# Clearing PSUM banks with a full stationary, and one value product in twelve moved from VectorE to ScalarE

## The chip, the cores and the metric

One NeuronCore of a Trainium2 chip runs the kernel. The metric is device time in microseconds of that core, from a launch to its end. Times of instructions come from one profiled execution; they count from the first instruction of its span.

## What is computed

A graph layer, an attention-like layer and a routed feed-forward layer over 1250 nodes of 512 features, with 21250 edges. The part that matters here is the graph layer, which the kernel turns into products with a dense, weighted adjacency matrix of 1250 x 1250:

```python
m = jnp.maximum(jnp.max(weighting_gate), 0.0)
exp_e = jnp.exp(weighting_gate - m)                       # one weight for each edge
row_sum = jax.ops.segment_sum(exp_e, src, num_segments=n_nodes)
atten_e = exp_e / (row_sum[src] + 1e-06)
Mfeat = source_features @ Wm + bm
out0 = jax.ops.segment_sum(atten_e[:, None] * Mfeat[dst], src, num_segments=n_nodes)
out1 = jax.ops.segment_sum(atten_e[:, None] * Mfeat[src], dst, num_segments=n_nodes)
h = jax.nn.relu(_layernorm(concatenate([out0, out1], -1) @ W1 + b1, gamma, beta))
...
x = x + _L0_gnn_ref(...) + _L0_mix_ref(...)               # then a routed feed-forward layer on top
```

## The kernel before, in words

The program is written engine by engine, each with its own instruction order, and semaphores between them. Its stages, in order: edges are sorted into buckets, and their records scattered to memory by GpSimd while the projections and the attention-like layer run on the other engines (to about 200 us); the last edges are sorted by products (L656, to 232 us); **the adjacency stage** (239 to 338 us); scaling and turning of the adjacency matrix and the products with the node features (L705, L712, L730 on); the routed feed-forward layer from 430 us on.

The adjacency stage builds 50 tiles of the matrix, each 125 source rows by 250 destination columns, and one column more for row sums. The sorted edge slots stand in 216 chunks of 128, one slot to a partition; each chunk belongs to one tile. 216 chunks are 108 pairs (PAIRS), and the pairs lie in 28 batches (BATCHES, L95): 26 of four pairs (PB), then two of two.

- **VectorE** makes the operands of a batch (L1190 to L1208): `s_one`, a one-hot of the source row (L1196), 128 columns for each chunk; `d_hot`, a one-hot of the destination column (L1200), 250 for each; and three products of `s_one` with a part of the edge's weight (L1207). The weight is split into WT = 3 parts of 16 bits (`parts[:, 2]` to `[:, 4]`), since the operands are bf16. A four-pair batch has 1024 columns in each of `s_one` and the three `s_hot`. `s_one` has two buffers, `d_hot` and `s_hot` have four (DB); VectorE waits for its own work (`one_ok`, `batch_ok`) and, from the fifth batch on, for TensorE's products of the batch four before (`chunk_ps`).
- **TensorE** takes pair by pair (L676 to L695). For each pair it first clears the bank in which a new tile begins, or an idle bank if none begins: a product of zeros with one column (L685), whose start flag makes the next products overwrite. The bank is in a register, computed from a table (`new_at`). The stationary of this product is one row of ones. Then come six products of 251 columns (L693), three weight parts for each of two chunks, into a bank that again a register gives. It waits for `batch_ok` before a batch's first product, and before a pair's clearing for `win_ok`, the copies up to the third pair before.
- **ScalarE** copies, for each pair, two tiles' worth (502 columns) out of PSUM to the matrix `adj` (L1525), to an idle place where no tile ended; the places are in registers, which are loaded anew from `at_i` once in four pairs (L1512). When all 108 copies are done VectorE sums the rows (L1213) and takes reciprocals, ScalarE (L1531) and VectorE scale the matrix, and TensorE begins to turn it (L705).

```python
pe.matmul(flat_banks[:, bass.ds(at_new, 1)], ones_row, zero_col, start=True, stop=False,
          skip_group_check=True)
...
for j in range(2):
    ...
    for i in range(WT):
        mm = pe.matmul(flat_banks[:, bass.ds(at_in, AW)], s_hot[:, n % DB, i, q, :, j],
                       d_hot[:, n % DB, q, :, j], start=False, stop=(i == WT - 1), skip_group_check=True)
```

Nothing plans the order: it is as the loops are written. The functions below hold the whole stage; the constant named `before` is a 128 x 128 matrix of 0 and 1 in 16 bits, whose first column is zero.

Of the kernel before, what the change touches and what calls it, by code (L numbers as in the profile page):

```python
# [16 lines left out]
TP, NT = 125, 10  # L17
# [84 lines left out]
def build(nc, x, edge_src, edge_dst, edge_w, consts, halves, biases, small, fold, wqkv, wp, bvt, w1f, w2f, b2f, out):  # L102
    with ExitStack() as ctx:
# [37 lines left out]
        ones_row, zero_col = half("ones")[0:1, :], half("before")[0:1, 0:1]  # L141
# [61 lines left out]
        parts = place("parts", 33728, [128, 2 + WT, NCH], BF16)  # L203
        d_hot = place("d_hot", 16064, [128, DB, PB, AW, 2], BF16)
# [101 lines left out]
        def piece(a, i):  # L306
# [21 lines left out]
        zeros_set, top_col, top_row, top_val, top_bc, top_sb, w_exp = (  # L328
            sem("zeros_set"), sem("top_col"), sem("top_row"), sem("top_val"), sem("top_bc"), sem("top_sb"), sem("w_exp"))
# [4 lines left out]
        fold_ps, fold_hi, fold_ok, foldb_ok = sem("fold_ps"), sem("fold_hi"), sem("fold_ok"), sem("foldb_ok")  # L334
# [3 lines left out]
        stat_ok, sum_ok, var_ok, std_ok, rstd_ok, xn_ok, xT_ps, xT_ok = (  # L338
            sem("stat_ok"), sem("sum_ok"), sem("var_ok"), sem("std_ok"), sem("rstd_ok"), sem("xn_ok"), sem("xT_ps"), sem("xT_ok"))
        q_ps, k_ps, v_ps, m_ps = sem("q_ps"), sem("k_ps"), sem("v_ps"), sem("m_ps")  # L340
        q_got, k_got, v_ok, m_ok = sem("q_got"), sem("k_got"), sem("v_ok"), sem("m_ok")
        top_ok, exp_ok, soft_ok, qT_ps, qT_ok, ctx_ps, ctx_ok, ctx_ok1, ctxd_zero = (
            sem("top_ok"), sem("exp_ok"), sem("soft_ok"), sem("qT_ps"), sem("qT_ok"), sem("ctx_ps"), sem("ctx_ok"),
            sem("ctx_ok1"), sem("ctxd_zero"))
# [6 lines left out]
            sem("col_ok"), sem("one_ok"), sem("batch_ok"), sem("chunk_ps"), sem("win_ok"))  # L351
        rinv_ok, even_ok, odd_ok, turn_ps, turn_a, turn_v, out_split = (
# [6 lines left out]
        var2_ok, std2_ok, x2T_ps, x2T_ok, log_ps, log_ok, lexp_ok, oh_ok, rank_ps = (  # L359
            sem("var2_ok"), sem("std2_ok"), sem("x2T_ps"), sem("x2T_ok"), sem("log_ps"),  # L360
            sem("log_ok"), sem("lexp_ok"), sem("oh_ok"), sem("rank_ps"))
        fac_ok, fac_st, tab_ok, ctab_ps, id_ok, exp_of = (
            sem("fac_ok"), sem("fac_st"), sem("tab_ok"), sem("ctab_ps"), sem("id_ok"), sem("exp_of"))
# [119 lines left out]
        def _(pe):  # L483
# [14 lines left out]
            pe.wait_ge(top_val, 1)  # L498
            pe.matmul(bank[4][0:TP, 0:1], ones[0:1, 0:TP], top[0:1, 2:3], start=True, stop=True).then_inc(top_bc, 1)
# [35 lines left out]
            def project(t):  # L535
                pe.wait_ge(xT_ok, t + 1)
                pe.wait_ge(xT_lo_ok, t + 1)
                for b, a, n, free, done in ((3, 0, D, q_got, q_ps), (4, D, D, k_got, k_ps),
# [6 lines left out]
                    if t == 0 and b == 4:  # L545
                        pe.wait_ge(foldb_ok, 1)
                    if t == 0 and b == 5:
                        pe.wait_ge(fold_ok, 2)
# [47 lines left out]
            pe.wait_ge(ctx_ok, 1)  # L596
# [79 lines left out]
            for p in range(PAIRS):  # L676
# [11 lines left out]
                if p == BATCHES[n][0]:  # L688
                    pe.wait_ge(batch_ok, n + 1)
# [1047 lines left out]
```

## Time and profile before

| | |
|---|---|
| median of 3 runs | 523.14 us (523.12 to 523.48) |
| the profiled execution | 522.98 us, span 520.7 us |
| mean granted TensorE clock over the span | 0.961 |
| TensorE products busy | 464.6 us, 89% |
| TensorE weight loads busy | 372.4 us, 72% |
| VectorE busy | 414.9 us, 80% |
| ScalarE busy | 256.7 us, 49% |
| GpSimd busy | 198.8 us, 38% |

How to read it: the span runs from the first to the last instruction; the execution's own time has 2.3 us more. Shares are means over stages with quite different limits, so a change inside one stage has to be judged by the rows of that stage. TensorE has two rows, since weight loads overlap products. A clock of 1.00 is 2.4 GHz, 0.50 is 1.2 GHz.

### The profile page before, as it was taken

To read this page: it belongs to the slowest core of one execution; us is meant where nothing else is said; L and a number is where in the kernel's file an instruction comes from. 1 tells how busy PE (TensorE), PEld (TensorE's weight loads), DVE (VectorE), ACT (ScalarE), POOL (GpSimd) and SP (SyncE) were. 2 spreads that over 40 slices of the span, in tenths; PEclk is the share of its full clock that TensorE was granted. 3 is DMA by queue.
4 is the path that set the end of the run, shared out by engine and by line. 5 is a ranking of instruction groups with operands and counts; after the bars stand their busy time and mean duration, and the time that the engine had idled before them with its cause. 6 is when DMAs were issued, how large, how long until landed. Compare 5 with 4: busy or idle time off the path is not lost.

```text
span 520.7 us, 8981 instructions
## 1 busy us (share of the span) xinstructions
PE 464.6 (89%) x2877; PEld 372.4 (72%) x2877; DVE 414.9 (80%) x793; ACT 256.7 (49%) x682; POOL 198.8 (38%) x159
## 2 busy tenths in 40 slices
PE   4189999999988999989999999989999847999992
PEld 1167878888867887967666666588988745788881
DVE  6969999999988887979999999578639857265562
ACT  0596566666661110003666666675345482466650
POOL 0088878688876888840000000000000006345322
PEclk9789999999999999999999999989999957899998
DMA  7980000000000000013000000000003992343210
GB/s 188 292 284 3 1 3 2 3 3 2 3 1 2 3 1 3 2 34 148 1 2 1 2 2 2 1 1 0 1 1 103 432 311 66 100 119 102 85 60 15
DMA packets 15840, 31.08 MB, mean 60 GB/s; under 512 B 7750, under 2 KB 8381, under 8 KB 14773
## 3 DMA queue, kind: packets, MB, share of 16 engines
q1 hardware_dynamic: 9237, 23.21, 13.3%
q0 software_dynamic: 6560, 7.32, 7.2%
q8 instruction: 25, 0.41, 0.3%
q14 instruction: 18, 0.15, 0.1%
HBM read 24.90 MB, written 7.38 MB: 62 GB/s over the span
## 4 chain that ended last, share of the span: by engine, by line
PE 40%; POOL 32%; issue 11%; DVE 8%; DMA 4%; SPq 3%; ACT 2%; DVEq 0%; POOLq 0%; ACTq 0%
POOL slots L454 31%; PE banks L693 16%; PE banks L840 6%; PE banks L532 5%; PE banks L712 3%; SPq L375 2%; PE banks L685 2%; PE banks L705 2%; PE banks L831 1%; PE banks L494 1%; DMA x_rows<-factors 1%; DVE rec L1274 1%; DVE stat L1276 1%; DMA rec<-x_rows,get_i 1%; PE banks L850 1%
## 5 line engine op out<-in xcount | busy, mean ns | idle before, releaser
L454 POOL DMA_INDIRECT slots<-record,row_i x120 | 161.6, 1346 | 68.4 <-issue 68.4
L465 POOL DMA_INDIRECT rec<-x_rows,get_i x17 | 20.0, 1176 | 207.0 <-DMA x_rows<-factors 202.1
L693 PE MATMUL banks<-d_hot,s_hot 128*128 128x251 bf16 x648 | 92.1, 276 | 0.9 <-DVE s_hot L1207 0.9
L1525 ACT ACTIVATE adj<-banks x108 | 63.7, 590 | 37.0 <-PE banks L693 36.8
L693 PEld LDWEIGHTS banks<-d_hot,s_hot 128*128 128x128 bf16 x648 | 54.4, 98 | 9.5 <-issue 1.0
L532 PE MATMUL banks<-w_hi,xT_hi 128*125 128x512 f32 (+1 forms) x160 | 59.5, 372 | 0.8 <-DVE bia L1045 0.4
L532 PE MATMUL banks<-w_hi,xT_lo 128*125 128x512 f32 (+1 forms) x160 | 58.6, 366 | 0.0
L532 PE MATMUL banks<-w_lo,xT_hi 128*125 128x512 f32 (+1 forms) x160 | 58.5, 366 | 0.0
L1207 DVE TENSOR_TENSOR s_hot<-s_one,parts 128x1024 bf16<-128x1024 bf16 (+1 forms) x84 | 51.0, 656 | 0.0
L1470 ACT ACTIVATE q_sb<-q_sb,hmax 125x64 f32<-125x64 f32 x80 | 26.7, 336 | 39.8 <-DVE hmax L1064 39.8
L532 PEld LDWEIGHTS banks<-w_hi,xT_hi 128*125 128x125 f32 x160 | 29.7, 185 | 7.1 <-issue 1.6
L532 PEld LDWEIGHTS banks<-w_hi,xT_lo 128*125 128x125 f32 x160 | 29.7, 185 | 5.6
L532 PEld LDWEIGHTS banks<-w_lo,xT_hi 128*125 128x125 f32 x160 | 29.7, 186 | 5.6
L473 POOL DMA_INDIRECT out<-o_sb,out_i x17 | 16.9, 994 | 41.4 <-DVE o_sb L1375 41.4
L1370 DVE TENSOR_TENSOR y_sb<-banks,b_sb 128x512 f32<-128x512 f32 x17 | 11.8, 691 | 26.1 <-PE banks L532 26.1
L1200 DVE TENSOR_TENSOR d_hot<-col,parts 128x2000 bf16<-128x2000 bf16 (+1 forms) x28 | 32.1, 1146 | 0.0
L656 PE MATMUL banks<-chunk_1h,row_1h 125*128 125x216 bf16 x250 | 26.0, 258 | 3.1 <-DVE row_1h L1142 2.0
L656 PEld LDWEIGHTS banks<-chunk_1h,row_1h 125*128 125x128 bf16 x250 | 23.2, 97 | 6.0 <-DVE row_1h L1142 4.5
L685 PEld LDWEIGHTS banks<-hlf 1*128 1x128 f16 x108 | 9.8, 90 | 23.6 <-issue 23.6
L1470 ACT ACTIVATE k_sb<-k_sb,hmax 125x64 f32<-125x64 f32 x80 | 26.6, 334 | 0.0
L712 PE MATMUL banks<-adj,msg 125*128 125x250 f32 x100 | 23.2, 378 | 0.0
L1496 ACT ACTIVATE xT_hi<-banks 128x500 fp32r<-128x500 f32 x10 | 5.9, 588 | 34.2 <-PE banks L617 34.2
(299 smaller groups left out, 1065.9 us busy)
## 6 DMA issues: line engine op xcount, KB each, us to landing
w_raw<-in_w2f SPq DMA_DIRECT2D x4, 1024.0 KB, 9.1
w_raw<-in_wqkv SPq DMA_DIRECT2D x3, 1024.0 KB, 18.9
rec<-in_x SPq DMA_DIRECT2D x2, 1120.0 KB
x_rows<-rec SPq DMA_DIRECT2D x10, 224.0 KB
w1a<-in_w1f SPq DMA_DIRECT2D x1, 2048.0 KB, 8.5
w1b<-in_w1f SPq DMA_DIRECT2D x1, 2048.0 KB, 16.6
b_sb<-in_b2f SPq DMA_DIRECT2D x1, 2048.0 KB, 22.2
slots<-record,row_i POOLq DMA_INDIRECT x120, 2.6
```

The lines of the kernel that those rows point to most:

```text
L454: pool.indirect_dma_start(slots, bass.IndirectOffsetOnAxis(ap=row_i[:, c:c + 1], axis=0), record[:, c, :], None).then_inc(slot_st, 16)
L465: pool.indirect_dma_start(rec_c[:, c % RING, :], None, x1_rows, bass.IndirectOffsetOnAxis(ap=get_i[:, c:c + 1], axis=0)).then_inc(ld_rec[c ...
L532: mm = pe.matmul(dst, ab, cd, start=(i == 0), stop=(i == n - 1))
L656: mm = pe.matmul(bank[1][:, k * NCH:(k + 1) * NCH], row_1h[:, n % RS, v, :, j], chunk_1h[:, n % RS, :, j], start=(n == 0 and j == 0 and v ...
L685: pe.matmul(flat_banks[:, bass.ds(at_new, 1)], ones_row, zero_col, start=True, stop=False, skip_group_check=True)
L693: mm = pe.matmul(flat_banks[:, bass.ds(at_in, AW)], s_hot[:, n % DB, i, q, :, j], d_hot[:, n % DB, q, :, j], start=False, stop=(i == WT - ...
L712: pe.matmul(hid_at(w), msg[:, t, GH:MD], adjw[:, t, w, 0:WIN], start=(t == 0), stop=False, skip_group_check=True)
L840: mm = pe.matmul(bank[1][:, 0:F], xsT[:, c % 2, k, :], w1_sb[k // 2][:, k % 2, bass.ds(e * F, F)], start=(k == 0), stop=(k == KD - 1))
L1200: dve.tensor_tensor(d_hot[:, r, 0:k, 0:WIN, :], col_2[:, :, :].unsqueeze(1).to_broadcast([128, k, WIN, 2]), values(1).to_broadcast([128, k ...
L1207: last = dve.tensor_tensor(s_hot[:, r, i, 0:k, :, :], s_one[:, n % 2, 0:k, :, :], values(2 + i).to_broadcast([128, k, CH, 2]), ALU.mult)
L1470: last = act.activation(ah, ah, ACT.Exp, bias=hmax[:, i, h:h + 1], accum_out=hsum[:, i, h:h + 1])
L1525: act.activation(adj[:, bass.ds(w, BW2)], flat_banks[0:TP, bass.ds(out_at, BW2)], ACT.Copy).then_inc(win_ok, 1)
```

## The change

1. The clearing product of each pair takes the whole 128 x 128 constant `before` as its stationary and that constant's first column, which is zero in all 128 rows, as the moving operand. It still clears, and still adds nothing.
2. For the batches 1 to 25, VectorE makes the third value product only for the first three pairs (768 of 1024 columns). ScalarE makes the fourth pair's: two products of 128 columns, one for each chunk, in 16 bits, with the 32-bit third part `low_f` as a scale from a pointer. They stand in ScalarE's order before the copy of the third pair of the batch before. `low_f` is computed once, by VectorE, behind batch 0.
3. TensorE waits for `act_hot` before a batch's fourth pair; VectorE waits for it before it overwrites `s_one`; ScalarE waits for `one_ok` and, from batch 4 on, for `chunk_ps`.
4. To make room for the two new semaphores, several that counted one event each are merged: `top_val` into `top_col`, `top_bc` into `top_row`, `foldb_ok` into `fold_ok`, `ctx_ok1` into `ctx_ok`, `oh_ok` and `tab_ok` into `route_ok`, `rank_ps` and `ctab_ps` into `route_ps`; `stat_ok` becomes a step of VectorE's own counter. Each wait stands where it stood.

```diff
-        ones_row, zero_col = half("ones")[0:1, :], half("before")[0:1, 0:1]
+        before, zero_col = half("before"), half("before")[:, 0:1]
...
+        low_f = place("low_f", 34272, [128, NCH])
...
                 if p >= 3:
                     pe.wait_ge(win_ok, p - 2)
-                pe.matmul(flat_banks[:, bass.ds(at_new, 1)], ones_row, zero_col, start=True, stop=False,
+                pe.matmul(flat_banks[:, bass.ds(at_new, 1)], before, zero_col, start=True, stop=False,
                           skip_group_check=True)
                 n, q = batch_of(p)
                 if p == BATCHES[n][0]:
                     pe.wait_ge(batch_ok, n + 1)
+                if q == PB - 1 and n >= 1:
+                    pe.wait_ge(act_hot, n)
...
                 if n >= 2:
                     dve.wait_ge(batch_ok, n - 1)
+                if n >= 3:
+                    dve.wait_ge(act_hot, min(n - 2, len(BATCHES) - 3))
...
                 for i in range(WT):
-                    last = dve.tensor_tensor(s_hot[:, r, i, 0:k, :, :], s_one[:, n % 2, 0:k, :, :],
-                                             values(2 + i).to_broadcast([128, k, CH, 2]), ALU.mult)
+                    m = k - 1 if i == WT - 1 and k == PB and n >= 1 else k
+                    last = dve.tensor_tensor(s_hot[:, r, i, 0:m, :, :], s_one[:, n % 2, 0:m, :, :],
+                                             values(2 + i)[:, 0:m, :, :].to_broadcast([128, m, CH, 2]), ALU.mult)
                 last.then_inc(batch_ok, 1)
+                if n == 0:
+                    dve.tensor_tensor(low_f[:, :], rest[:, :], parts[:, 3, :], ALU.subtract).then_inc(low_ok, 1)
...
+            def low_hot(n):
+
+                c = 2 * BATCHES[n][1] - 2
+                act.wait_ge(one_ok, n + 1)
+                if n >= DB:
+                    act.wait_ge(chunk_ps, BATCHES[n - DB][1])
+                for j in range(2):
+                    last = act.activation(s_hot[:, n % DB, WT - 1, PB - 1, :, j], s_one[:, n % 2, PB - 1, :, j], ACT.Copy,
+                                          scale=low_f[:, c + j:c + j + 1])
+                last.then_inc(act_hot, 1)
+
             read_at(from_at, 4, 0)
             for p in range(PAIRS):
+                if p == 2:
+                    act.wait_ge(low_ok, 1)
+                if p % PB == 2 and p + PB < PAIRS - PB:
+                    low_hot(p // PB + 1)
```

ScalarE's order at the start of the stage, before (ISA rows compute places from registers, TENSOR_LOAD fills the registers):

```order
L1512 TENSOR_LOAD at_i
L1520 ISA
L1525 ISA [waits chunk_ps]
L1525 ACTIVATE adj<-banks 125x502
L1520 ISA
L1525 ISA [waits chunk_ps]
L1525 ACTIVATE adj<-banks 125x502
L1520 ISA
L1525 ISA [waits chunk_ps]
L1525 ACTIVATE adj<-banks 125x502
```

and of the change (its lines are numbered otherwise: L1548 is the copy, L1529 the new product):

```order
L1520 TENSOR_LOAD at_i
L1543 ISA
L1548 ISA [waits chunk_ps]
L1548 ACTIVATE adj<-banks 125x502
L1543 ISA
L1548 ISA [waits chunk_ps]
L1548 ACTIVATE adj<-banks 125x502
L1529 ACTIVATE s_hot<-s_one,low_f 128x128 [waits one_ok,low_ok]
L1529 ACTIVATE s_hot<-s_one,low_f 128x128
L1543 ISA
L1548 ISA [waits chunk_ps]
L1548 ACTIVATE adj<-banks 125x502
```

Two products now stand between the second and the third copy, and so in each of the first 25 batches.

VectorE's order in a batch of the steady part (the fourth batch), before:

```order
L1196 TENSOR_TENSOR s_one<-col_91,parts 128x1024 [waits batch_ok]
L1200 TENSOR_TENSOR d_hot<-col_91,parts 128x4x500
L1207 TENSOR_TENSOR s_hot<-s_one,parts 128x1024 [waits one_ok]
L1207 TENSOR_TENSOR s_hot<-s_one,parts 128x1024 x2
L1196 TENSOR_TENSOR s_one<-col_91,parts 128x1024 [waits batch_ok]
```

and of the change (L1201, L1205, L1213 in place of L1196, L1200, L1207):

```order
L1201 TENSOR_TENSOR s_one<-col_91,parts 128x1024 [waits act_hot,batch_ok]
L1205 TENSOR_TENSOR d_hot<-col_91,parts 128x4x500
L1213 TENSOR_TENSOR s_hot<-s_one,parts 128x1024 [waits one_ok]
L1213 TENSOR_TENSOR s_hot<-s_one,parts 128x1024
L1213 TENSOR_TENSOR s_hot<-s_one,parts 128x768
L1201 TENSOR_TENSOR s_one<-col_91,parts 128x1024 [waits act_hot,batch_ok]
```

The third value product is shorter, and the one-hot of the rows has one wait more.

## Rows read from the trace of the kernel before

**Rows 1.** The chain of waits from 238 to 345 us, its share by line.

```profile
by line: PE banks L693 79.3%; PE banks L685 10.5%; PE banks L705 2.3%; PE banks L712 2.3%; DVE s_hot L1207 1.8%; issue 1.4%; ACT adj L1531 1.3%; ACT adj L1525 0.6%; DVE parts L1204 0.4%; DVE rs L1213 0.2%; DVE rinv L1215 0.2%; DVE rse L1214
```

**Rows 2.** Stretches: us; PE, PEld, DVE, ACT, POOL busy; TensorE clock; DMA.

```profile
216.00:231.00 15.00, 13.02 (x120) 10.49 (x118) 14.38 (x33) 0.00 (x0) 10.65 (x8) 1.00 0.07 3
241.00:337.00 96.00, 95.86 (x754) 64.07 (x755) 91.73 (x135) 62.96 (x107) 0.00 (x0) 1.00 0.01 2
337.00:345.00 8.00, 5.03 (x24) 4.49 (x22) 4.83 (x10) 5.94 (x8) 0.00 (x0) 0.79 0.01 2
```

**Rows 3.** Timeline: start us, length us, ..., [idle before]; L693 by source line, min/median/max.

```profile
270.71 1.26 ACT L1525 ACTIVATE adj<-banks  x2 [0.52 <-PE banks L693]
271.17 0.09 PEld L685 LDWEIGHTS banks<-hlf 1*128 1x128 f16 x1 [0.22 <-issue]
271.17 0.17 PE L685 MATMUL banks<-hlf 1*128 1x1 f16 x1
271.27 0.57 PEld L693 LDWEIGHTS banks<-d_hot,s_hot 128*128 128x128 bf16 x6
271.28 0.86 PE L693 MATMUL banks<-d_hot,s_hot 128*128 128x251 bf16 x6
...
272.07 0.17 PE L685 MATMUL banks<-hlf 1*128 1x1 f16 x1
...
272.27 0.59 ACT L1525 ACTIVATE adj<-banks  x1 [0.31 <-PE banks L693]
L693 PE MATMUL banks<-d_hot,s_hot x648: 272/274/290, 241.1 to 337.0; 128*128 128x251 bf16 x162
```

**Rows 4.** Who waited for whom from 241 to 337 us: total, times, longest.

```profile
PEld banks L685 <- issue: 23.3, 107, 0.4
```

**Rows 5.** VectorE's timeline, batch 1 and the start of batch 2.

```profile
240.82 0.68 DVE L1196 TENSOR_TENSOR s_one<-col,parts 128x1024 bf16<-128x1024 bf16 x1
...
242.54 1.89 DVE L1207 TENSOR_TENSOR s_hot<-s_one,parts 128x1024 bf16<-128x1024 bf16 x3
244.34 0.68 DVE L1196 TENSOR_TENSOR s_one<-col,parts 128x1024 bf16<-128x1024 bf16 x1
```

**Rows 6.** VectorE's timeline, its last batches.

```profile
327.60 1.27 DVE L1207 TENSOR_TENSOR s_hot<-s_one,parts 128x1024 bf16<-128x1024 bf16 x2
...
329.73 1.08 DVE L1207 TENSOR_TENSOR s_hot<-s_one,parts 128x512 bf16<-128x512 bf16 x3
330.73 0.41 DVE L1196 TENSOR_TENSOR s_one<-col,parts 128x512 bf16<-128x512 bf16 x1
```

**Rows 7.** TensorE's timeline, its first and its last pair.

```profile
241.05 0.84 PE L693 MATMUL banks<-d_hot,s_hot 128*128 128x251 bf16 x6 [0.88 <-DVE s_hot L1207]
...
336.43 0.85 PE L693 MATMUL banks<-d_hot,s_hot 128*128 128x251 bf16 x6
```

**Rows 8.** Ten short products of L820, and the product behind them, in the timeline.

```profile
429.47 0.44 PE L820 MATMUL banks<-chunk_tag,row_hot 125*128 125x17 f16 x10 [4.35 <-DVE chunk_tag L1348]
429.75 0.77 PE L823 MATMUL banks<-cst 128*128 128x250 f32 x1
```

**Rows 9.** A 216-column difference of VectorE, by source line.

```profile
L1204 DVE TENSOR_TENSOR parts<-rest,parts x1: 379/379/379, 238.6 to 238.6; 128x216 bf16<-128x216 f32 x1
```

**Rows 10.** ScalarE: pointer products and register loads by source line, copies in the timeline.

```profile
L1470 ACT ACTIVATE q_sb<-q_sb,hmax x80: 331/333/350, 43.1 to 150.3; 125x64 f32<-125x64 f32 x80
L1531 ACT ACTIVATE adj<-adj,rinv x5: 1321/1337/1349, 338.8 to 357.6; 125x1250 f32<-125x1250 f32 x5
L1512 ACTq TENSOR_LOAD <-at_i x28: 313/550/761, 236.9 to 333.9; - x28
345.59 1.34 ACT L1537 ACTIVATE adjT_hi<-banks 125x500 fp32r<-125x500 f32 x3 [1.21 <-PE banks L705]
```

**Rows 11.** Turning products behind the stage, TensorE's timeline, at low and at full clock.

```profile
340.26 2.43 PE L705 MATMUL banks<-cst,adj 125*125 125x125 f32 x10 [2.97 <-ACT adj L1531]
...
344.96 1.25 PE L705 MATMUL banks<-cst,adj 125*125 125x125 f32 x10
```

More of the change, by code:

```diff
@@ L351, in build @@
             sem("col_ok"), sem("one_ok"), sem("batch_ok"), sem("chunk_ps"), sem("win_ok"))
+        act_hot, low_ok = sem("act_hot"), sem("low_ok")
         rinv_ok, even_ok, odd_ok, turn_ps, turn_a, turn_v, out_split = (
@@ L497, in _ @@
             mm.then_inc(count_ps, 1)
-            pe.wait_ge(top_val, 1)
-            pe.matmul(bank[4][0:TP, 0:1], ones[0:1, 0:TP], top[0:1, 2:3], start=True, stop=True).then_inc(top_bc, 1)
+            pe.wait_ge(top_col, 2)
+            pe.matmul(bank[4][0:TP, 0:1], ones[0:1, 0:TP], top[0:1, 2:3], start=True, stop=True).then_inc(top_row, 1)
             pe.wait_ge(count_ok, 1)
@@ L545, in project @@
                     if t == 0 and b == 4:
-                        pe.wait_ge(foldb_ok, 1)
+                        pe.wait_ge(fold_ok, 1)
                     if t == 0 and b == 5:
-                        pe.wait_ge(fold_ok, 2)
+                        pe.wait_ge(fold_ok, 3)
                     split_product(bank[b][0:TP, 0:n],
@@ L595, in _ @@
                          ).then_inc(own_ps, 1)
-            pe.wait_ge(ctx_ok, 1)
-            pe.wait_ge(ctx_ok1, 1)
+            pe.wait_ge(ctx_ok, 2)
             pe.wait_ge(qT_ok, NT)
@@ L806, in _ @@
             both(route, 4)
-            pe.wait_ge(oh_ok, 1)
+            pe.wait_ge(route_ok, 1)
             for t in range(NT):
@@ L815, in _ @@
                            start=False, stop=True, skip_group_check=True)
-            mm.then_inc(rank_ps, 1)
-            pe.wait_ge(tab_ok, 1)
+            mm.then_inc(route_ps, 1)
+            pe.wait_ge(route_ok, 2)
             for t in range(NT):
                 mm = pe.matmul(bank[6][:, 0:NC], row_hot[:, t, :], chunk_tag[:, t, :], start=(t == 0), stop=(t == NT - 1))
-            mm.then_inc(ctab_ps, 1)
+            mm.then_inc(route_ps, 1)
             for _ in range(MOE_UP):
@@ L913, in _ @@
                     own_step(dve.tensor_reduce(top[0:1, 1:2], bank[3][0:1, 0:TP], X, ALU.max))
-                    dve.tensor_scalar(top[0:1, 2:3], top[0:1, 1:2], 0.0, -1.0, ALU.max, ALU.mult).then_inc(top_val, 1)
+                    dve.tensor_scalar(top[0:1, 2:3], top[0:1, 1:2], 0.0, -1.0, ALU.max, ALU.mult).then_inc(top_col, 1)
             dve.scalar_tensor_tensor(s_lo[:, :], s_hi[:, :], -float(TP), src_i[:, :], ALU.mult, ALU.add)
@@ L924, in _ @@
             dve.memset(prs[:, 2, :], 0.0)
-            dve.wait_ge(top_bc, 1)
+            dve.wait_ge(top_row, 2)
             dve.tensor_copy(top[:, 3:4], bank[4][0:TP, 0:1]).then_inc(top_sb, 1)
@@ L982, in _ @@
             for t in range(DT):
-                norm_stats(t)
+                last = norm_stats(t)
+            own_step(last)
             def chunk_tables():
@@ L1044, in _ @@
             dve.wait_ge(fold_ps, 2)
[L1045 removed]
+            dve.tensor_copy(bias("m"), bank[4][0:TP, 0:MD]).then_inc(fold_ok, 1)
             low_part(2)
@@ L1317, in _ @@
             own_step(dve.tensor_reduce(best[:, :], eq[:, :, :], X, ALU.max))
-            dve.tensor_tensor(oh16[:, :, :], prefer, over_e(best[:, :]), ALU.is_equal).then_inc(oh_ok, 1)
+            dve.tensor_tensor(oh16[:, :, :], prefer, over_e(best[:, :]), ALU.is_equal).then_inc(route_ok, 1)
             dve.tensor_tensor(oh[:, :, :], prefer, over_e(best[:, :]), ALU.is_equal)
```

34 lines of the change are left out of this document (16 added, 18 removed).

## The prediction, made before the changed kernel ran

> **What bounds the kernel now.** I read four views. First the chain of waits over the stage that the change touches, 238 to 345 us: 79.3% of it is the 251-column products of L693 and 10.5% the one-column clearing products of L685 [rows 1]. So TensorE's stream of pairs is the path there. Second the busy time by stretch [rows 2]: from 241 to 337 us TensorE is busy 95.86 of 96 us, but VectorE 91.73 and ScalarE 62.96. Two engines are nearly full, and the question is which is next if one gets faster. Third the timeline inside the stage, for one pair of chunks. Its six products start at 271.28 and take 0.86; less the 0.274 that one lasts, the last starts 0.59 after the first, at 271.87. The next clearing starts at 272.07, 0.20 behind that, and a first product 0.11 behind its clearing (271.17 to 271.28) [rows 3]. The period is 0.59 + 0.20 + 0.11 = 0.90; over the whole stage it is (336.43 - 241.05)/107 = 0.89 [rows 7]. In the list of waits the weight queue stands idle before L685 for 23.3 us in 107 times, 0.22 each, and the cause is "issue": no semaphore and no engine was late [rows 4]. Between the other products nothing stands idle, since their weights are loaded beside the running product: six loads in 0.57 us under six products [rows 3].
>
> Fourth, VectorE's step, from one start to the next: the two one-hots 242.54 - 240.82 = 1.72, the three value products 244.34 - 242.54 = 1.80, so 0.60 each; a batch of four pairs is 3.52 us [rows 5]. TensorE's four pairs are 4 x 0.89 = 3.56. **The two run nearly level.** VectorE's last full batch is ready at 327.60 + 1.27 = 328.87 [rows 6], and TensorE starts its last product at 336.43 + 0.85 - 0.27 = 337.01 [rows 7].
>
> **The change, part by part.** *Clearing products.* The stationary goes from one row to 128, in 108 products; the moving operand stays one column. The trace has no one-column product with a full stationary. Nearest are ten products of L820, 125 rows, 16 bits, 17 columns, each with a load: 0.44 us for ten, less 0.17 that a short one lasts, is 0.03 from start to start; and the 32-bit product of L823 behind them starts at 429.75, 0.02 after the tenth, so neither a new data type nor a new line makes a gap [rows 8]. At the floor, then, the clearing starts 0.11 behind the last product (0.57 of loads for six is 0.10 each, and 0.59/5 is 0.12; a product's step over the stage is (0.89 - 0.31)/5 = 0.116) and the next product 0.03 behind it: 0.14 in place of 0.31. The ceiling, if the gap goes, is that the clearing steps like a full product: 0.22. A pair becomes 0.58 + 0.14 = 0.72 or 0.80; I take 0.72, since one column is nearer to 17 than to 251. Beyond the ceiling lies the case that the gap stays (4 below).
> The Trainium skill, page TensorEngine Tiling (Array Packing), section Tiling Modes, says that a change of the tiling mode, as from 32 rows to 128, drains the array; by it the gap goes in full. Another page speaks against it: TensorE: Matmul & The Clock Gate, section Part 3, has weight loads overlap running products only where their row groups differ, so that a 128-row load would stand in line. The trace does not bear that out: the loads of rows 3 run beside products of the same rows.
>
> *VectorE.* In 25 of 28 batches the third value product shrinks from 1024 to 768 columns. With 1024 it steps 0.60, with 512 (330.73 - 329.73)/3 = 0.33 [rows 6]; half way is 0.467, so 0.133 is saved and a batch is 3.39. In all 25 x 0.133 = 3.33. Added is one difference of 216 columns behind batch 0: 0.38 [rows 9], less the 0.08 by which a product's duration exceeds its step, so 0.30. Net 3.03. The new wait there (act_hot) looks two batches back, at work done several us before; I price it at zero. If ScalarE ran that late, the one-hot of the rows, and all of VectorE behind it, would be late with it.
>
> *ScalarE* gets two 128-column products in 25 batches, with a scale from a pointer. Nearest are 64 columns with a pointer, 0.333, and 1250 with one, 1.337: on the line between, 0.387. Two of them overlap by some 0.10, as three copies of 500, 500 and 250 columns do, which take 1.34 [rows 10] where they would take 0.59, 0.59 and some 0.38 alone (a column is 0.85 ns between those two rows); so a batch gets 0.58 more, at most 0.77. The 502-column copies last 0.59. Their step is 0.48 at best, by the same row, and 0.67 at worst (two in 1.26, [rows 3]). One step in a batch holds a register load of 0.55, at most 0.76 [rows 10]; it fits in 0.89 now, so 1.10 for the longest. Low: 3 x 0.48 + 0.89 + 0.58 = 2.91. High: 3 x 0.67 + 1.10 + 0.77 = 3.88. The middle is 3.4; but 0.67 and 0.89 were still paced by TensorE, so I take 3.1, nearer the low end, **under VectorE's 3.39**. What waits behind the two products is the copy of the third pair. A copy starts 0.40 behind its pair's last product (271.87 and 272.27) and ends 0.99 behind it [rows 3]; TensorE needs it for the clearing three pairs on, 2 x 0.72 + 0.11 = 1.55 behind, so 0.56 of delay is covered. Without that cover the two products would add to every batch.
>
> *TensorE's rest.* It waits for act_hot before each fourth pair; that part was made during the batch before. The merged semaphores leave each wait in its place; zero.
>
> **The sum.** A batch starts 0.15 after its last product: batch 0's ended 0.08 behind 240.82, TensorE began at 241.05 [rows 5, 7]. New batch times: TensorE 4 x 0.72 + 0.15 = 3.03, VectorE 3.39. **VectorE becomes the bound**, up to its last full batch, ready at 328.87 - 3.03 = 325.84. TensorE begins it at 325.99 and is at it until 328.9. The first half batch, made in 329.73 + 1.08 - 328.87 = 1.94, is ready at 327.8, before that; the second at 329.7, before TensorE has done the first (330.3). So eight pairs run without a stop, and the last product starts at 325.99 + 7 x 0.72 + 0.58 = 331.61. Before it was 337.01. **Gain 5.4 us**; all behind it (last copy, row sums, scaling, turning) hangs on that copy and moves along. The profiled execution took 522.98 us, for a span of 520.7, and stands 0.16 below the median of 523.14; with the gain it would be 517.6, the median 517.7. With the ceiling for the clearing (0.80 a pair) TensorE's batch is 3.35, still under VectorE's, and only the tail is 7 x 0.08 longer: 518.3.
>
> **What could go otherwise.**
> 1. *The clock behind the stage.* TensorE stood idle from 337.3 to 340.26, and then ran at 1.2 GHz for a while (0.79 of 2.4 in the mean over 337 to 345 us [rows 2]): ten turning products took 2.43 against 1.25 later, so 1.2 us [rows 11]. The idle time stays 3 us long but moves; if the low stretch falls into it, 1.2 is gained on top: 516.5. Inside the stage TensorE will idle 0.4 of each 3.4 us; from 216 to 231 us it was busy 13.02 of 15 at clock 1.00 [rows 2], so I expect no loss there.
> 2. *ScalarE is the bound, at a batch between 3.39 and 3.56.* Half of that is 25 x 0.085 = 2.1 given back: 519.9. Its high end of 3.88 speaks for it, its 33 idle us of 96 against.
> 3. *Slower: ScalarE above 3.56 a batch.* The place is the copy behind the two products and the register load; it decides from 3.56 up, where TensorE stands now. At 3.68, between middle and high, it is 25 x 0.12 = 3.0 more than now: 526.
> 4. *The gap stays*, since it belongs to the one-column product or to the computed address and not to the row count. Then TensorE keeps 0.89, VectorE's saving only lengthens its lead, and the fuller load costs at most 0.01 more, 108 times (0.10 against 0.09, [rows 3]): 523.1 to 524.2. L820's short products without a gap speak against.
>
> **Chances.** Forecast 0.62, clock 0.17, ScalarE near the bound 0.11, gap stays 0.06, slower 0.04. About 0.2% (1.05 us) is what a measurement of this kernel tells from no change. The first three are faster, 0.90; the fourth is the same, 0.06; slower 0.04. The range runs from the clock case, 516.2 with its rounding, over the forecast and its ceiling to the middle of the ScalarE case, 519.8.
>
> **What would show it.** Right: the clearing 0.11 behind the last product and the next product 0.03 behind it; no "issue" idle time before it; TensorE idle once in a batch, for 0.4, released by s_hot; VectorE's one-hots of the rows 3.39 apart; the last product near 331.6. Wrong: pairs still 0.89 apart (4); TensorE waiting for win_ok or act_hot while ScalarE is busy without a break (2, 3); 768-column products that step 0.6.

## The result, and the profile after

| | before | changed |
|---|---|---|
| first runs, median | 523.31 us (523.12 to 523.57, 4 runs) | 516.90 us (515.5 to 519.31, 4 runs) |
| ratio, 95% interval | | 0.9882 (0.9843 to 0.9921) |
| second set, median | 522.90 us (519.33 to 525.23, 16 runs) | 517.68 us (514.07 to 520.27, 11 runs) |
| ratio, 95% interval | | 0.9899 (0.9871 to 0.9927) |
| the profiled execution | 522.98 us, span 520.7 | 519.31 us, span 517.2 |
| mean granted TensorE clock | 0.961 | 0.954 |

The change is faster, by 1.0 to 1.2%. Single executions of either kernel are up to 6 us apart, so that for what the stage itself does the profile says more than a median: from the first one-hot of the rows to the start of the last 251-column product it took 337.01 - 236.88 = 100.13 us before. Changed, it starts at 236.01 and ends as this timeline of TensorE shows (start us, length us, engine, line, operation, count, idle time before):

```profile
330.17 0.84 PE L696 MATMUL banks<-d_hot,s_hot 128*128 128x251 bf16 x6
333.99 2.44 PE L708 MATMUL banks<-cst,adj 125*125 125x125 f32 x10 [2.97 <-ACT adj L1554]
336.22 4.12 PE L715 MATMUL banks<-adj,msg 125*128 125x250 f32 x10
340.18 1.25 PE L708 MATMUL banks<-cst,adj 125*125 125x125 f32 x10
```

The last product starts at 330.17 + 0.84 - 0.27 = 330.74, so the stage took 330.74 - 236.01 = 94.73 us: **5.40 us less**. In line numbers of the changed kernel, L696 is the product with 251 columns, L686 the clearing, L708 and L715 the turning and the inward products behind the stage. The ten L715 products took 4.12 us, against 2.28 at full clock in a run below.

The chain of waits from 238 to 345 us is no longer TensorE's [rows 1]:

```profile
by line: DVE s_hot L1213 43.3%; issue 21.2%; DVE s_one L1201 14.1%; PE banks L715 6.0%; PE banks L696 5.5%; PE banks L708 4.3%; DVE d_hot L1205 2.7%; ACT adj L1554 1.3%; ACT adj L1548 0.6%; DVE parts L1209 0.4%; DVE low_f L1217 0.3%; DVE rs
```

VectorE's value products and its one-hots lead it. The 21.2% of "issue" are VectorE's too: in each batch they lie between the one-hot of the rows and the first value product, 0.93 us in which, by its timeline, it makes `d_hot`. The busy time by stretch (us; PE, PEld, DVE, ACT, POOL busy; TensorE clock; DMA) says the same: TensorE busy 81.46 of 90, VectorE 87.83, and the clock at 1.00 in the stage [rows 2]:

```profile
241.00:331.00 90.00, 81.46 (x750) 64.54 (x746) 87.83 (x134) 71.93 (x157) 0.00 (x0) 1.00 0.01 2
331.00:345.00 14.00, 11.03 (x54) 10.03 (x54) 8.29 (x16) 8.17 (x14) 0.00 (x0) 0.76 0.00 1
```

Inside the stage, the timeline of one batch and of the next one's start. L1201 makes the one-hots of the rows, L1213 the value products, L1529 is ScalarE's new product, L1548 its copy:

```profile
269.12 0.85 PE L696 MATMUL banks<-d_hot,s_hot 128*128 128x251 bf16 x6
...
269.81 0.16 PE L686 MATMUL banks<-hlf 128*128 128x1 f16 x1
269.81 0.57 PEld L696 LDWEIGHTS banks<-d_hot,s_hot 128*128 128x128 bf16 x6
269.83 0.84 PE L696 MATMUL banks<-d_hot,s_hot 128*128 128x251 bf16 x6
269.87 0.72 ACT L1529 ACTIVATE s_hot<-s_one,low_f 128x128 bf16<-128x128 bf16 x2
270.46 1.05 ACT L1548 ACTIVATE adj<-banks  x2
...
270.70 0.70 DVE L1201 TENSOR_TENSOR s_one<-col,parts 128x1024 bf16<-128x1024 bf16 x1
...
270.94 0.85 PE L696 MATMUL banks<-d_hot,s_hot 128*128 128x251 bf16 x6 [0.24 <-DVE s_hot L1213]
...
274.08 0.71 DVE L1201 TENSOR_TENSOR s_one<-col,parts 128x1024 bf16<-128x1024 bf16 x1
...
274.28 0.17 PE L686 MATMUL banks<-hlf 128*128 128x1 f16 x1 [0.36 <-ACT adj L1548]
```

Read it against [rows 3] and [rows 5]. The last product of a pair starts at 269.12 + 0.85 - 0.27 = 269.70, the clearing at 269.81 and the first product behind it at 269.83: 0.11 and 0.02 in place of 0.20 and 0.11. VectorE's one-hots come at 270.70 and 274.08, 3.38 apart in place of 3.52. TensorE waits once a batch: at 270.94 for VectorE (0.24), and in the next batch at 274.28, at the clearing (0.36; the part on why the prediction was right comes back to it). ScalarE's two new products take 0.72 together, and the next copy starts 0.59 behind the start of the first.

Who waited for whom from 241 to 331 us (total us, times, longest), three of the lines, beside the one with 23.3 us in 107 times before [rows 4]:

```profile
PEld banks L686 <- issue: 9.1, 17, 0.7
...
PE banks L686 <- ACT adj L1548: 4.4, 11, 0.5
PE banks L696 <- DVE s_hot L1213: 3.8, 13, 0.7
```

The weight queue still stands idle before the clearing, but 17 times and not 107, each time at the start of a batch. Between the pairs inside a batch it is not idle.

### The profile page after: what moved, and what is told of

The parts are those of the page before. It is cut to its first block, busy times and chain, and to the rows that moved or that the text cites. A ratio compares the mean times of both kernels' runs of the same rounds, so it can differ in the third digit from the quotient of the medians.

```text
span 517.2 us, 9080 instructions
## 1 busy us (share of the span) xinstructions
PE 453.7 (88%) x2877; PEld 374.8 (72%) x2877; DVE 412.1 (80%) x794; ACT 265.5 (51%) x732; POOL 197.6 (38%) x159
## 4 chain that ended last, share of the span: by engine, by line
POOL 32%; PE 24%; DVE 20%; issue 15%; DMA 4%; SPq 2%; ACT 2%; DVEq 0%; POOLq 0%; ACTq 0%
POOL slots L456 31%; DVE s_hot L1213 9%; PE banks L843 7%; PE banks L534 5%; PE banks L715 3%; DVE s_one L1201 3%; SPq L377 2%; PE banks L708 2%; PE banks L834 1%; DMA x_rows<-factors 1%; PE banks L496 1%; DVE rec L1282 1%; PE banks L696 1%; DVE stat L1284 1%; DMA rec<-x_rows,get_i 1%
## 5 line engine op out<-in xcount | busy, mean ns | idle before, releaser
L696 PE MATMUL banks<-d_hot,s_hot 128*128 128x251 bf16 x648 | 80.1, 275 | 4.8 <-DVE s_hot L1213 4.8
L1548 ACT ACTIVATE adj<-banks x108 | 60.5, 585 | 22.8 <-PE banks L696 18.9
L696 PEld LDWEIGHTS banks<-d_hot,s_hot 128*128 128x128 bf16 x648 | 55.0, 97 | 15.0 <-issue 6.1
L1213 DVE TENSOR_TENSOR s_hot<-s_one,parts 128x1024 bf16<-128x1024 bf16 (+2 forms) x84 | 48.7, 653 | 0.0
L1205 DVE TENSOR_TENSOR d_hot<-col,parts 128x2000 bf16<-128x2000 bf16 (+1 forms) x28 | 33.1, 1182 | 0.0
L715 PE MATMUL banks<-adj,msg 125*128 125x250 f32 x100 | 24.7, 396 | 0.0
L1231 DVE TENSOR_TENSOR adjT_lo<-banks,adjT_hi 125x500 fp32r<-125x500 f32 (+1 forms) x30 | 16.0, 585 | 9.5 <-ACT adjT_hi L1560 9.3
```

Source lines behind the costliest of these rows:

```text
L715: pe.matmul(hid_at(w), msg[:, t, GH:MD], adjw[:, t, w, 0:WIN], start=(t == 0), stop=False, skip_group_check=True)
L1205: dve.tensor_tensor(d_hot[:, r, 0:k, 0:WIN, :], col_2[:, :, :].unsqueeze(1).to_broadcast([128, k, WIN, 2]), values(1).to_broadcast([128, k ...
L1213: last = dve.tensor_tensor(s_hot[:, r, i, 0:m, :, :], s_one[:, n % 2, 0:m, :, :], values(2 + i)[:, 0:m, :, :].to_broadcast([128, m, CH, 2] ...
L1548: act.activation(adj[:, bass.ds(w, BW2)], flat_banks[0:TP, bass.ds(out_at, BW2)], ACT.Copy).then_inc(win_ok, 1)
```

## The experiments

"Stage" is the stretch defined above, from each kernel's profile, and "pair" the step from pair to pair inside a batch. "Behind" is the time from the start of the last 251-column product to the start of the second tile's turning, in the same profile. The stage repeats within 0.1 us over the five profiles whose stage is the change's own (changed, change_again, fill_stage, fill_both, fill_both_again: 94.72 to 94.82). Whole times are medians beside runs of the kernel before on the same chip.

| run | stage us | VectorE batch | pair | behind us | whole time, ratio (95%) |
|---|---|---|---|---|---|
| before | 100.13 | 3.52 | 0.89 | 7.95 |  |
| changed | 94.73 | 3.38 | 0.72 | 9.44 | 0.9882 (0.9843 to 0.9921) |
| clear_only | 97.84 | 3.52 | 0.72 | 6.53 | 0.9949 (0.9928 to 0.997) |
| act_only | 100.34 | 3.39, then up to 3.57 | 0.89 | 9.47 | 1.0004 (0.9979 to 1.0029) |
| rows_64 | 100.50 | 3.39, then up to 3.58 | 0.89 | 7.94 | one run, 522.08 us |
| rows_96 | 94.76 | 3.39 | 0.72 | 8.11 | one run, 517.00 us |
| two_pairs | 97.27 | 3.25, then 3.48 | 0.72 to 0.82 | 8.19 | one run, 520.51 us |
| change_again | 94.73 | 3.39 | 0.72 | 8.21 | 0.9899 (0.9871 to 0.9927) |
| fill_stage | 94.82 | 3.39 | 0.72 | 6.53 | 0.9862 (0.9818 to 0.9905) |
| fill_both | 94.72 | 3.39 | 0.72 | 6.53 | 0.9844 (0.9807 to 0.9882) |
| fill_both_again | 94.73 | 3.39 | 0.72 | 6.54 | 0.9824 (0.9787 to 0.9861) |
| before_fill | 101.31 | 3.52 | 0.89 | 6.54 | 0.9962 (0.9937 to 0.9987) |
| pool_pair | 95.93 | 3.44 | 0.72 | 6.53 | 0.9899 (0.9861 to 0.9937) |
| pool_fill | 96.04 | 3.44 | 0.72 | 6.53 | 0.9856 (0.9827 to 0.9885) |

### The two halves, each alone

clear_only is the kernel before with only this:

```diff
-        ones_row, zero_col = half("ones")[0:1, :], half("before")[0:1, 0:1]
+        before, zero_col = half("before"), half("before")[:, 0:1]
```

> The kernel before, with the full 128-row stationary in the clearing products and nothing else. Theory (the gap goes with the one-row stationary, and VectorE is then the bound at 3.52 us a batch): pairs 0.71 apart inside a batch, TensorE idle some 0.5 us once in a batch, one-hots of the rows still 3.52 apart; the last product 2.4 us earlier than before, measured from the first one-hot of the rows (97.7 us behind it in place of 100.1). Rival (VectorE was not level with TensorE, and the clearing alone brings it all): 5.4 us earlier. In the whole time some 2.4 us less, if the clock behind the stage behaves as before.

Stage 97.84, 2.3 less than before, whole time 0.9949. Its timeline at two places:

```profile
300.70 0.68 DVE L1196 TENSOR_TENSOR s_one<-col,parts 128x1024 bf16<-128x1024 bf16 x1
...
300.92 0.84 PE L693 MATMUL banks<-d_hot,s_hot 128*128 128x251 bf16 x6 [0.52 <-DVE s_hot L1207]
...
304.22 0.68 DVE L1196 TENSOR_TENSOR s_one<-col,parts 128x1024 bf16<-128x1024 bf16 x1
...
334.21 0.84 PE L693 MATMUL banks<-d_hot,s_hot 128*128 128x251 bf16 x6
```

Here the wait for VectorE is 0.52 and the one-hots are still 3.52 apart. The clearing alone hands the stage to VectorE after 2.3 us; the rival that it brings everything is out.

act_only is the changed kernel with that line turned back:

```diff
-        before, zero_col = half("before"), half("before")[:, 0:1]
+        ones_row, zero_col = half("ones")[0:1, :], half("before")[0:1, 0:1]
```

> The changed kernel with the old one-row stationary: only ScalarE's share of the third value part. Theory: TensorE stays the bound at 0.89 a pair, VectorE's one-hots come 3.38 apart until its four buffers are full and then wait; the last product 100.1 us behind the first one-hot, as before, within 0.3 us. Rival (VectorE's length counted, the clearing not): 3.0 us earlier. Whole time within 0.5 us of before.

Stage 100.34 and ratio 1.0004: no gain. Two of its waits over 241 to 337 us:

```profile
PEld banks L686 <- issue: 23.4, 107, 0.4
...
DVE s_one L1201 <- ACT s_hot L1529: 1.5, 1, 1.5
```

The 23.4 us of "issue" idle time are back; VectorE ran 3.39 us batches up to the 21st, had then filled its buffers, and fell to TensorE's 3.56. So the halves alone give 2.3 and -0.2 us, together 5.4: each removed what had kept the other's gain from showing.

### Which property of the clearing product made the gap

rows_64 and rows_96 are the changed kernel with fewer rows in the clearing:

```diff
-        before, zero_col = half("before"), half("before")[:, 0:1]
+        before, zero_col = half("before")[0:64, :], half("before")[0:64, 0:1]
```

and the same with `0:96`.

> The changed kernel with 64 rows in the clearing's stationary and moving operand. Theory (the gap comes when the group of rows that a product uses changes between fewer and all 128): pairs 0.89 apart as with one row, last product about 100 us behind the first one-hot. Rival (what counts is that the load has a full-size, fast form, or simply more than one row): pairs 0.71 apart, 94.7 us.

> The changed kernel with 96 rows in the clearing's stationary and moving operand. Theory (more than 64 rows count as the whole array, as the products with 125 rows elsewhere do): pairs 0.71 apart, last product 94.7 us behind the first one-hot. Rival (only exactly the same rows as the neighbours' 128 avoid the gap): 0.89 apart.

With 64 rows the gap is back in full. First the timeline, then the clearing's own line (count: shortest, median and longest ns); the idle time before it, all of it "issue", is 23.5 us in 108 times:

```profile
300.23 0.85 PE L696 MATMUL banks<-d_hot,s_hot 128*128 128x251 bf16 x6
301.01 0.17 PE L686 MATMUL banks<-hlf 64*128 64x1 f16 x1
301.12 0.85 PE L696 MATMUL banks<-d_hot,s_hot 128*128 128x251 bf16 x6
...
L686 PE MATMUL banks<-hlf x108: 171/174/174, 239.1 to 335.8; 64*128 64x1 f16 x108
```

The clearing starts 0.20 behind the last product (300.23 + 0.85 - 0.27 = 300.81) and the next product 0.11 behind the clearing, as with one row. With 96 rows the gap is gone, by the timeline:

```profile
299.79 0.85 PE L696 MATMUL banks<-d_hot,s_hot 128*128 128x251 bf16 x6
300.48 0.17 PE L686 MATMUL banks<-hlf 96*128 96x1 f16 x1
300.50 0.84 PE L696 MATMUL banks<-d_hot,s_hot 128*128 128x251 bf16 x6
```

A clearing product lasts 0.174 with 64 rows and 0.164 with 128; its column count, its data type and its computed address are the same in all of them. The stationary and the moving operand have the same rows, so what makes the gap is the number of rows that the product uses: going from 128 rows to 64 or fewer and back costs it, going to 96 and back does not. Between 64 and 96 nothing was tried. The Trainium skill, page TensorEngine Tiling (Array Packing), section Tiling Modes, has 32 and 64 rows as modes of their own and a drain at each change of mode; these two runs agree, with 0.17 us a pair for the two changes. The rule of the Trainium skill, page TensorE: Matmul & The Clock Gate, section Part 3, that a load runs beside a product only if their row groups differ, does not hold here: the six loads from 269.81 on take 0.57, within the 0.84 of six products of the same 128 rows.

### How much ScalarE has left

two_pairs lets ScalarE make two pairs' third part:

```diff
-                    m = k - 1 if i == WT - 1 and k == PB and n >= 1 else k
+                    m = k - 2 if i == WT - 1 and k == PB and n >= 1 else k
...
-                for j in range(2):
-                    last = act.activation(s_hot[:, n % DB, WT - 1, PB - 1, :, j], s_one[:, n % 2, PB - 1, :, j], ACT.Copy,
-                                          scale=low_f[:, c + j:c + j + 1])
+                for j in range(4):
+                    q, i = PB - 2 + j // 2, j % 2
+                    last = act.activation(s_hot[:, n % DB, WT - 1, q, :, i], s_one[:, n % 2, q, :, i], ACT.Copy,
+                                          scale=low_f[:, c + j:c + j + 1])
```

TensorE's wait for `act_hot` moves to the third pair with it.

> The changed kernel with ScalarE making the third value part of two pairs of a batch in place of one. VectorE's batch is 0.13 shorter, 3.25. Theory (ScalarE has little left: four copies at least 0.47 apart, four products of 0.31 to 0.43, one register load): it becomes the bound, batches between 3.5 and 3.9 us, stage 97 to 107 us, TensorE waiting for act_hot or win_ok. Rival (ScalarE has room, as its 20% of idle time says): batches 3.25, stage 91.5 us.

VectorE's batches are 3.25 for the first thirteen; then its buffers are full and they are 3.48. ScalarE's timeline in the second part, and a line of the waits of the stage:

```profile
309.80 1.31 ACT L1530 ACTIVATE s_hot<-s_one,low_f 128x128 bf16<-128x128 bf16 x4
...
312.80 0.59 ACT L1549 ACTIVATE adj<-banks  x1 [0.27 <-PE banks L696]
313.28 1.30 ACT L1530 ACTIVATE s_hot<-s_one,low_f 128x128 bf16<-128x128 bf16 x4
...
PE banks L686 <- ACT adj L1549: 3.8, 11, 0.7
```

ScalarE's round is 313.28 - 309.80 = 3.48, where I had 3.5 to 3.9, and the stage of 97.27 lies at the low end of the 97 to 107 expected. But ScalarE is not busy without a break: it waits 0.27 us of this round for TensorE's products, and TensorE waits for its copies (3.8 us, 11 times). So the bound is the loop of the two and not ScalarE's work alone. The rival was right for half the stage. One pair is a better share for ScalarE than two: the second costs 2.5 us.

### GpSimd as a third maker

pool_pair keeps ScalarE's pair and gives the third pair's third part to GpSimd:

```diff
+            pool.wait_ge(low_ok, 1)
+            for n in range(1, len(BATCHES) - 2):
+                c = 2 * BATCHES[n][1] - 4
+                pool.wait_ge(one_ok, n + 1)
+                if n >= DB:
+                    pool.wait_ge(chunk_ps, BATCHES[n - DB][1])
+                for j in range(2):
+                    last = pool.tensor_scalar(s_hot[:, n % DB, WT - 1, PB - 2, :, j], s_one[:, n % 2, PB - 2, :, j],
+                                              low_f[:, c + j:c + j + 1], None, ALU.mult)
+                last.then_inc(pool_hot, 1)
```

with a wait for `pool_hot` on TensorE before the third pair and on VectorE before `s_one`.

> The changed kernel, and GpSimd, which is idle in this stage, makes the third value part of the third pair in batches 1 to 25 (two products of 128 columns with a scale from a pointer); ScalarE keeps the fourth pair. Theory (VectorE is the bound of the stage, ScalarE has some 0.2 us left in a batch): VectorE's batch 3.25, stage 94.7 - 25 x 0.133 = 91.4 us, whole time 3.3 us below the changed kernel. Rivals: GpSimd's and VectorE's accesses get in each other's way, so that VectorE's steps grow and the stage stays at 94 or more; or ScalarE becomes the bound at 3.3 to 3.4, stage 92.5 to 94.

The first rival came true. Timeline of the two engines:

```profile
269.74 0.77 DVE L1215 TENSOR_TENSOR s_one<-col,parts 128x1024 bf16<-128x1024 bf16 x1
...
270.43 1.19 DVE L1219 TENSOR_TENSOR d_hot<-col,parts 128x2000 bf16<-128x2000 bf16 x1
...
270.60 3.08 POOL L467 TENSOR_SCALAR s_hot<-s_one,low_f 128x128 bf16<-128x128 bf16 x2 [0.36 <-DVE s_one L1215]
...
271.54 1.71 DVE L1227 TENSOR_TENSOR s_hot<-s_one,parts 128x1024 bf16<-128x1024 bf16 x3
...
273.18 0.77 DVE L1215 TENSOR_TENSOR s_one<-col,parts 128x1024 bf16<-128x1024 bf16 x1
```

GpSimd takes 3.08 us for two products of 128 columns, and VectorE's batch is 273.18 - 269.74 = 3.44, not 3.25: its one-hot of the rows steps 0.69 instead of 0.60 (270.43 - 269.74), and the three value products 1.64 where two at 0.60 and one of half size at 0.33 would be 1.53. Stage 95.93, 1.2 longer than the change. two_pairs is the control: there VectorE makes the same instructions without GpSimd, and its batch is 3.25 while the buffers have room. So GpSimd's products are what lengthens VectorE's; that it happens at their access to memory is argued, not shown, and how long GpSimd's products take beside an idle VectorE was not measured. The profile of this run has a span of only 510.6 us, 6.6 below the change's, although its stage is longer. It began the stage 1.35 earlier (234.66 against 236.01), and behind the stage its clock stayed at 1.00, so that the second turning came 6.53 behind the last product and not 9.44; the rest lies further on. One whole time says little here. The median is no better than the change's (ratio 0.9899 for both).

### The clock behind the stage

In the changed kernel's profile TensorE stood idle from 331.0 to 333.99, and the clock was granted at 0.76 over 331 to 345 us. The ten turning products at 333.99 took 2.44 as before, but the ten inward ones took 4.12, so the second tile's turning began 340.18 - 330.74 = 9.44 behind the last product; before it was 344.96 - 337.01 = 7.95 [rows 7, 11]. Of the 5.4 us gained, 1.5 were lost again in this execution.

First the changed kernel again, unedited:

> The changed kernel once more, unedited, to see its spread beside the others of this call. Theory (the stage gives 5.4 us, and the rest of a run's difference is which stretches run at 1.2 GHz): the stage 94.7 us long in this profile again, and single times between 515.5 and 519.5 us with the kernel before within 0.5 us. Rival (the stage itself varies): a stage length off by over 0.3 us.

The stage is 94.73 again. Its single times went from 514.07 to 520.27, and those of the kernel before from 519.33 to 525.23, both wider than I had expected; the median over eleven runs is 517.68. The turning products behind the stage now took 1.33 and the inward ones 3.96, by the row by stretch and by TensorE's timeline:

```profile
331.00:345.00 14.00, 11.44 (x61) 10.33 (x62) 9.85 (x19) 9.23 (x14) 0.00 (x0) 0.88 0.00 1
...
333.56 1.33 PE L708 MATMUL banks<-cst,adj 125*125 125x125 f32 x10 [2.97 <-ACT adj L1554]
334.73 3.96 PE L715 MATMUL banks<-adj,msg 125*128 125x250 f32 x10
```

fill_stage keeps TensorE busy there:

```diff
+            for _ in range(FILL):
+                pe.matmul(bank[0][:, 0:WIN], ident, const("cols"), start=True, stop=True)
             pe.wait_ge(mix_ok, NT)
             pe.wait_ge(win_ok, PAIRS)
```

with FILL = 6. The expectation, then the row by stretch and TensorE's timeline:

> The changed kernel with 6 products of the identity with a constant (two passes each, 0.21 a pass, 2.5 us together) into a bank that nobody reads, behind the last pair, where TensorE otherwise stands idle for 3 us. Theory (the idle time lets the clock fall, and the fall costs 1.2 to 2.7 us in the turning and the first inward products): no stretch at 1.2 GHz within 10 us behind the stage, ten L715-like products in 2.3 us; whole time 1.2 to 2.7 us below the changed kernel. Rival (the clock falls for what happened earlier, inside the stage, where TensorE is idle 0.4 us in a batch): the fall stays and nothing is gained.

```profile
331.00:345.00 14.00, 13.56 (x84) 12.32 (x84) 10.04 (x19) 10.20 (x17) 0.00 (x0) 1.00 0.01 1
...
330.94 2.69 PE L720 MATMUL banks<-cst 128*128 128x250 f32 x12
334.08 1.32 PE L709 MATMUL banks<-cst,adj 125*125 125x125 f32 x10 [0.44 <-ACT adj L1557]
335.25 2.28 PE L716 MATMUL banks<-adj,msg 125*128 125x250 f32 x10
337.36 1.25 PE L709 MATMUL banks<-cst,adj 125*125 125x125 f32 x10
```

Here L720 is the fill, L709 the turning and L716 the inward products. Clock 1.00 over the whole stretch, ten inward products 2.28, second turning 337.36 - 330.83 = 6.53 behind the last product: 2.9 us earlier than in the change's first profile, 1.7 than in its second. The median is 516.15 against 517.68 of change_again, and their intervals overlap, so the times do not show the gain and one profile does not either. For two kernels without a fill have the same 6.53: pool_pair, and clear_only, of which this is the row by stretch from its last product on:

```profile
335.00:349.00 14.00, 11.03 (x72) 10.34 (x72) 10.05 (x20) 10.20 (x17) 0.00 (x0) 1.00 0.01 1
```

Counted over all profiles (column "behind"): without a fill the clock fell behind the stage in seven of nine, at 7.94 to 9.47; with the fill it fell in none of five, at 6.53 or 6.54. By chance alone that would come about once in a hundred. Inside the stage it was 1.00 in all fourteen, in the changed kernel's too, where TensorE waits once a batch. So the fall belongs to TensorE's 3 us of idle time behind the stage and not to the short ones inside, but that idle time does not bring it every time, and why two executions escaped is open. Where it does, the fill saves 1.4 to 2.9 us.

before_fill is the control, the same six products in the kernel before.

> The kernel before with the same 6 products behind the last pair as in fill_stage, as a control. Theory (what they give has nothing to do with the change: also before, the clock falls behind the stage, 3.4 us long in the profile shown): stage 100.1 us long, no stretch at 1.2 GHz behind it, ten turning products and ten inward products in 3.3 us in place of 4.7, whole time 1.4 us below the kernel before. Rival (only the changed kernel, with TensorE idle inside the stage, gains): no difference.

Ratio 0.9962 (0.9937 to 0.9987): the fill is worth about 2 us there too, so it is a gain of its own. The ten turning and the ten inward products took 3.28 (342.99 - 339.71) in place of 4.70. The stage reads 101.31, off from the 100.1 expected: in this execution VectorE began at 235.15, and TensorE, busy until 240.4 with products that only keep it running ahead of the stage, started 240.45 - 235.15 = 5.30 behind it in place of 4.17, 1.1 late. From TensorE's first product to its last it is 96.00 against 95.96.

fill_both adds five more such products before the first expert chunk, `MOE_UP = 17` in place of 12.

> As fill_stage, and 17 in place of 12 such products before the first expert chunk. Theory: the fall to 1.2 GHz at the first expert products (10 us long in the changed kernel's profile) is later or shorter, since TensorE stands idle for 0.2 in place of 2.1 us before the first chunk's turning; 1 to 2.5 us less than fill_stage. Rival: the more products run at 1.2 GHz before the gather lands and end late, no gain or up to 1 us more.

A second set of the same kernel:

> fill_both once more, for an interval of its own beside fresh runs of the kernel before. Theory: stage 94.7 us again, no stretch at 1.2 GHz behind it, most single times between 513 and 516 us, some 2 to 3 us below the changed kernel's 517.7. Rival (its first set was lucky in how the clock fell at the expert products): median 516 or more.

And both fills with GpSimd's share:

> pool_pair with the fills of fill_both. Theory: both gains add, some 3 us below fill_both (514.6), near 511.5 us. Rival: as for pool_pair, no gain over fill_both.

The timeline of TensorE in the changed kernel at the start of the experts (L834 is the turning, L843 the first expert products):

```profile
433.85 0.63 PE L834 MATMUL banks<-cst,xs 128*128 128x128 f32 x4 [2.12 <-ACT xs L1645]
...
437.03 2.07 PE L843 MATMUL banks<-w1a,xsT 128*128 x4 [0.24 <-issue]
...
442.28 2.07 PE L843 MATMUL banks<-w1a,xsT 128*128 x4 [0.17 <-issue]
```

and in fill_both_again (L837 and L846 are the same two):

```profile
431.85 0.63 PE L837 MATMUL banks<-cst,xs 128*128 128x128 f32 x4 [0.54 <-ACT xs L1648]
...
434.94 1.13 PE L846 MATMUL banks<-w1a,xsT 128*128 x4 [0.61 <-issue]
...
438.40 1.13 PE L846 MATMUL banks<-w1a,xsT 128*128 x4 [0.41 <-issue]
```

In the first, TensorE was idle for 2.12 us before the turning, and each group of four L843 products took 2.07; in the second, idle for 0.54, and 1.13 each. From the first turning to the second chunk's group it is 442.28 - 433.85 = 8.43 against 438.40 - 431.85 = 6.55. Medians of 514.64 and 513.72 (0.9844 and 0.9824 of before) make this **the fastest version**, some 3 to 4 us below the change's 517.68; against change_again the interval of fill_both just overlaps (0.9882 and 0.9871), that of fill_both_again does not. In fill_both's own profile, though, the clock fell at the same place in spite of the fill, where TensorE was idle for 0.49 and 1.45 us before its first two turnings. At the first expert products the clock fell in one of the three profiles with the longer fill and in all eleven without it, so by these few profiles the fill makes the fall rarer there and does not exclude it. pool_fill misses its 511.5: its median is 515.32, its stage 96.04, and the rival (no gain over fill_both) came true.

## Why the prediction was right

The forecast of 517.7 us stands beside medians of 516.9 and 517.68, and the gain in the stage of 5.4 beside 5.40. The stage is what was worked out, and it came out part by part. VectorE's last full batch was ready 328.87 - 236.88 = 91.99 behind its first one-hot before, and 323.17 + 1.80 - 236.01 = 88.96 in the change:

```profile
323.17 1.80 DVE L1213 TENSOR_TENSOR s_hot<-s_one,parts 128x1024 bf16<-128x1024 bf16 x3
```

That is 3.03 less, as forecast. From there to the last product it took 8.14 before and 330.74 - 324.97 = 5.77 in the change, 2.37 less; the forecast has the same 5.77. The whole time agreeing to 0.02 us is luck: the interval of its ratio is 1.5 us to either side, and the first median is 0.8 away. By its steps:

- **The clearing.** Taken as 0.11 and 0.03, measured 0.11 and 0.02; a pair 0.72, measured 0.71 to 0.72 inside a batch. The rival that the gap belongs to the one-column product or the computed address is refuted by rows_64 and rows_96, which have both.
- **VectorE.** 0.133 saved by the shorter product and a batch of 3.39; measured 3.384 in the mean from the second one-hot of the rows to the 27th. That it would become the bound is what the chain says and clear_only confirms, with its one-hots still 3.52 apart; that VectorE's saving counts once the clearing is cheaper, and only then, is the point on which the 5.4 rests, and act_only, which has the saving alone and gains nothing, shows it. low_f was priced at 0.30; the first batch grew from 3.94 to 4.23, 0.29.
- **ScalarE.** This term was mis-sized: 0.387 a product by the line between two pointer products, measured 0.428 (shortest, median, longest ns, from the list by line of the changed kernel):

```profile
L1529 ACT ACTIVATE s_hot<-s_one,low_f x50: 423/428/437, 242.6 to 324.3; 128x128 bf16<-128x128 bf16 x50
```

  The two add 0.59 to its round, as taken (0.58), since one overlaps the next by 0.14 (they start 0.29 apart) and not by 0.10. That the two errors cancel is luck. Copies do come 0.47 apart where TensorE does not pace them, at the low bound of 0.48. ScalarE stayed under VectorE's round: it was busy 71.93 of 90 us, 2.70 a batch. The 3.1 that I took for its round no run tests.
- **The start of a batch.** Expected: TensorE idle 0.4 once a batch, released by s_hot. That holds in 13 cases. In 11 the wait falls at the clearing and is put down to ScalarE's copy. But the copy that this clearing needs is that of the third pair before it, and it had ended at 273.22 (two copies of 1.30 us together from 271.92 on), a microsecond earlier. What stands there on TensorE's own sequencer, by the list by line, is this:

```profile
L670 PEldq TENSOR_LOAD <-at_i x14: 587/1104/1120, 236.0 to 327.1; - x14
```

  It is the load of sixteen registers, once in two batches. At 272.92 it begins and lasts 1.10; products that were already issued run on, and the next pair's clearing follows at 274.28. I had counted ScalarE's register loads and not TensorE's. It cost the stage nothing: VectorE's batch was ready at 272.41 + 1.78 = 274.19 only, and TensorE began at 274.40, 0.07 later behind it than in the batch before (270.94, ready at 270.80). For a faster VectorE it is next in line.
- **The clock** was a rival with 17% and a gain of 1.2 at stake. It moved the profiled executions in both directions: in the first of the change it cost 1.5 more than before, and in clear_only and pool_pair it did not fall at all behind the stage. It moved them at the experts as well, which I had left out. The medians fell by 6.4 and 5.2 where the stage gives 5.4. The 0.2% that I took for what a measurement tells from no change, from three runs, was too small: sixteen runs of the kernel before spread over 5.9 us.

## What to carry to other kernels

When two engines run level in a stage, read both rounds before pricing a change: each alone gave 2.3 and -0.2 us here, and both 5.4. Idle time of TensorE's weight queue with no releaser ahead of one small product can be a sign that this product uses another number of the array's rows than its neighbours; if they use 128, give it 96 or more. And where the work behind a gap of 3 us is on the path, filling the gap with products that nobody reads is worth trying, with the granted clock of the stretch as the measure, over several profiles.

## What the runs showed of the hardware that I had not expected

- A change from products of 128 rows to one of 64 or of one row, and back, cost 0.17 us together; 64 rows cost as much as one, 96 as little as 128.
- Sixteen registers of TensorE took 1.10 us to load, eight 0.59, and nothing of its later work was issued meanwhile.
- GpSimd needed 1.07 to 2.05 us for a 128-column, 16-bit product beside a busy VectorE, where ScalarE needed 0.43.
- Single times of one kernel spread over 6 us on the same chip (514.07 to 520.27 for the change), while the length of this stage repeats within 0.1 us over five profiles. Executions differ in the stretches at 1.2 GHz behind the stage and at the first experts, and already ahead of the stage: its first one-hot starts between 234.66 and 237.27 in the fourteen profiles, and why is open.
